# Self-attention with the scores laid the other way round: keys on the partitions, the softmax sum from a column of ones, the output normalised on its way out of PSUM

## The reference, cut to what matters

```
xn = layernorm(x, g1)
q = xn @ Wq.T                      # 16 heads of 64
kv = xn @ Wkv.T                    # one k and one v of 64
q, k = l2norm(q * 16), l2norm(k)   # each then times sqrt(16)
sim = einsum('bhid,bjd->bhij', q, k), causal
attn = softmax(sim)
out = einsum('bhij,bjd->bhid', attn, v)
out = layernorm(out @ Wout.T, g2)
x = layernorm(x + out)
```

## Time and profile before

| what | value |
|---|---|
| median of 3 executions | 832.95 us (831.18 to 836.39) |
| the profiled execution | 833.86 us |
| its span, first to last instruction | 832.1 us |
| TensorE busy / weight loads | 770.5 us (93%) / 646.4 us (78%) |
| VectorE, ScalarE, GpSimd busy | 620.7 us (75%), 596.5 us (72%), 454.3 us (55%) |
| granted TensorE clock, mean | 0.987 of full speed |

### The profile page before, as it was taken

How to read it: one execution, slowest core, us unless ns; L and a number is a source line. 1 busy time by engine, 2 the same in 40 slices (tenths; PEclk the granted TensorE clock), 3 DMA queues, 4 the chain that set the end, 5 groups by cost and what they waited for, 6 DMA issues and landing times.

```text
span 832.1 us, 26529 instructions
## 1 busy us (share of the span) xinstructions
PE 770.5 (93%) x9276; PEld 646.4 (78%) x9308; DVE 620.7 (75%) x1834; ACT 596.5 (72%) x1444; POOL 454.3 (55%) x442
## 2 busy tenths in 40 slices
PE   3799999999999998899899999999999989989995
PEld 3577778777777877788788888887888878989962
DVE  3877878878877874789888888888888965744425
ACT  2688888878878874777778777676767667767735
POOL 6467776776777672222253535444443537776643
PEclk9899999999999999999999999999999989999998
DMA  8299999100000000000000000000000227878745
GB/s 273 67 159 165 162 161 156 16 0 0 0 0 0 0 3 2 6 7 7 7 22 17 23 17 20 20 20 20 16 23 14 72 76 225 254 221 250 248 157 210
DMA packets 69392, 64.79 MB, mean 78 GB/s; under 512 B 5702, under 2 KB 54985, under 8 KB 69168
## 3 DMA queue, kind: packets, MB, share of 16 engines
q1 hardware_dynamic: 62592, 51.42, 29.8%
q0 software_dynamic: 4624, 9.61, 3.3%
q10 hardware_dynamic: 2080, 2.49, 1.0%
HBM read 35.37 MB, written 28.58 MB: 77 GB/s over the span
## 4 chain that ended last, share of the span: by engine, by line
PE 47%; issue 19%; POOL 13%; DVE 9%; ACT 6%; DMA 3%; SPq 1%; POOLq 0%; DVEq 0%; ACTq 0%
PE bank L1715 7%; PE bank L1819 6%; PE bank L1515 5%; POOL rq L534 5%; PE bank L1517 5%; PE bank L1516 5%; POOL PR L539 3%; PE bank L1829 3%; PE bank L1703 3%; PE bank L1591 2%; PE bank L1599 2%; PE bank L1690 2%; ACT VBD L393 2%; DMA w_now<-in_wl 2%; POOL rs L548 1%
## 5 line engine op out<-in xcount | busy, mean ns | idle before, releaser
L393 ACT COPY VBD<-bank 64x512 f32<-64x512 f32 x192 | 111.4, 580 | 28.1 <-PE bank L1517 25.4
L571 POOL TENSOR_TENSOR PR<-PR,rL 128x1024 f32<-128x1024 f32 x32 | 60.9, 1904 | 107.9 <-DVE rL L1125 107.7
L534 POOL TENSOR_TENSOR rq<-ssq,mhalf 128x17 f32<-128x17 f32 x32 | 99.3, 3102 | 14.4 <-DVE ssq L974 13.8
L539 POOL TENSOR_TENSOR PR<-PR,rL 128x1024 f32<-128x1024 f32 x32 | 61.0, 1905 | 82.4 <-DVE rL L1005 82.4
L638 POOL DMA_INDIRECT zbuf<-arena x71 | 69.8, 983 | 31.6 <-issue 21.2
L626 POOL DMA_INDIRECT xbuf<-xg,slot x64 | 64.9, 1013 | 34.2 <-DVE xg L1320 21.6
L1819 PE MATMUL bank<-xT,w_now 128*128 128x128 f32 x568 | 77.3, 280 | 3.1 <-DMA w_now<-in_wl 2.7
L1819 PEld LDWEIGHTS bank<-xT,w_now 128*128 128x128 f32 x568 | 70.4, 195 | 4.6 <-issue 3.5
L1446 DVE SCALAR_TENSOR_TENSOR stage<-bank,b_now,early 128x128 f32<-128x128 f32 x142 | 43.3, 347 | 40.4 <-ACT early L892 32.6
L892 ACT ACTIVATE early<-bank,b_now 128x128 f32<-128x128 f32 x142 | 44.6, 365 | 35.8 <-PE bank L1819 35.7
L1715 PE MATMUL bank<-VBD,PT 128*64 128x128 f32 x1024 | 64.7, 280 | 3.2 <-ACT PT L808 3.2
(11 more groups left out here) (253 smaller groups left out, 2296.0 us busy)
## 6 DMA issues: line engine op xcount, KB each, us to landing
w_now<-in_wl SPq DMA_DIRECT2D x71, 256.0 KB
xbuf<-blank SPq DMA_DIRECT2D x1, 17160.0 KB, 119.6
arena<-xbuf SPq DMA_DIRECT2D x71, 65.0 KB
VBD<-zbuf SPq DMA_DIRECT2D x4, 512.0 KB, 5.0
out<-X SPq DMA_DIRECT2D x8, 256.0 KB, 2.3
cT<-in_ctxT ACTq DMA_DIRECT2D x16, 96.0 KB, 1.9
zbuf<-arena POOLq DMA_INDIRECT x71
wl_sb<-in_wl POOLq DMA_DIRECT2D x1, 1024.0 KB, 8.5
```

The lines of the kernel that those rows point to most:

```text
L393: u = copy(VBD[h * SEQ:(h + 1) * SEQ, p, s, lo:lo + blocks, :], bank[CHUNK_BANK[c]][s * SEQ:(s + 1) * SEQ, :].rearrange("k (a d) -> k a d" ...
L534: nc.gpsimd.tensor_tensor(rq[:, :], ssq[:, :], mhalf[:, 0:HEADS + 1], ALU.pow).then_inc(a["pow"], 1)
L539: nc.gpsimd.tensor_tensor(v, v, rL[:, p, :].unsqueeze(2).broadcast_to([P, HEADS, SEQ]), ALU.mult)\
```

## The change

It turns the scores round. The keys stand on the partitions now: four products of 64x64 corners with 512 columns (one per sequence and half of the heads) in place of 32 with 64 columns. The exponentials then are already the stationary operand of the product with the values, so that the transposes of the weights, ScalarE's copies of them and the block diagonal `VBD` go. v has a column of ones beside it (`kvS`, a ring of VB = 4 tiles), so that the 65th column of the product is the sum over the keys. The sum on VectorE, its reciprocal over 16 heads and GpSimd's multiply go; the new `o_norm` on VectorE takes the reciprocal of those columns and multiplies the output on its way out of PSUM. It lies with the queries on the partitions, so eight transposes on TensorE and two copies on ScalarE (`o_T`) follow before the projection, which works on each sequence by itself. Beside that: x, k and kv share bank 1 (with waits on `kvS`), the square sums, powers, caps and normalise steps are done by halves of the heads, the loop has four tiles, and y of the last two tiles goes to banks 2 and 3.

```diff
 def norms(t, p):                                        # GpSimd
+    for c in range(2):
+        s = half(c)
+        pool.wait_ge(a["ssq"], 2 * t + c + 1)
...
+        nc.gpsimd.tensor_tensor(rq[:, s], ssq[:, s], mhalf[:, s], ALU.pow).then_inc(a["pow"], 1)
-def weights(t, p):
-    pool.wait_ge(a["sum"], 2 * t + 2)
...
+def kv_evac(t, p):                                      # ScalarE
     act.wait_ge(a["kv"], t + 1)
     nc.scalar.activation(wide[:, W:W + DH], bank[1][:, 0:DH], ACT.Square).then_inc(a["sq"], 1)
+    nc.scalar.activation(kvS[:, p, 0:2 * DH], bank[1][:, 0:2 * DH], ACT.Copy).then_inc(a["kvS"], 1)
...
+def o_norm(t, p):                                       # VectorE
+    dve.wait_ge(a["o"], t + 1)
+    first = psum[:, 4:6, 0:O_LAST * O_W].rearrange("q s (a d) -> q s a d", d=O_W)
+    last = psum[:, 0:2, O_AT:O_AT + O_W]
+    V.reciprocal(rO[:, :, O_LAST:NBLK], last[:, :, DH:O_W]).then_inc(a["rO"], 1)
+    V.reciprocal(rO[:, :, 0:O_LAST], first[:, :, :, DH]).then_inc(a["rO"], 1)
...
+    V.tensor_tensor(On[:, :, O_LAST, :], last[:, :, 0:DH], ...)
+    for s in range(PB):
+        V.tensor_tensor(On[:, s, 0:O_LAST, :], first[:, s, :, 0:DH], ...)
...
 def qk_T(t, p):                                         # TensorE
...
     pe.wait_ge(a["kn"], t + 1)
+    pe.wait_ge(a["kvS"], upto_tile(t + 2))
+    nc.tensor.transpose(bank[1][:, KN_AT], kn[:, :, :].rearrange("q s d -> q (s d)"), ident[:, :])\
 def scores(t, p):
...
-                m = M(bank[6 + h][s * SEQ:(s + 1) * SEQ, k * SEQ:(k + 1) * SEQ],
-                      QT[r, p, k, s * SEQ:(s + 1) * SEQ], kT[r, p, s * SEQ:(s + 1) * SEQ],
-                      start=False, stop=(k == NBLK - 1))
+            m = M(bank[6 + h][q, :], kT[r, p, q], QT[r, p, :, q], start=False, stop=True)
...
-def values(t, p, s):
-    M(bank[4 + s][:, :], VBD[:, p, s, 0, :], PT[:, s * HW:(s + 1) * HW], start=True, stop=True)\
+def values(t, p):
+    for k in range(NBLK):
...
+        for s in range(PB):
+            rows = slice(s * SEQ, (s + 1) * SEQ)
+            for h in range(2):
...
+                m = M(to[h * SEQ:(h + 1) * SEQ, :], PR[rows, p % 2, at:at + SEQ], kvS[rows, p, V_ONE],
+                      start=True, stop=True)
+def o_T(t, p, s):
+    pe.wait_ge(a["on"], 3 * t + 2 + s)
...
 # order in a turn, TensorE
-stage_of(qkv, i, p, 0)
+self_stage(q_product, i, p, 0)
+self_stage(lambda t, q: o_T(t, q, 0), i, p, 3)
+self_stage(lambda t, q: o_T(t, q, 1), i, p, 3)
+self_stage(kv_product, i, p, 0)
```

More of the change, by code:

```diff
@@ L275, in pipeline @@
             for i in range(first):
[L276 to L281, removed]
+                body(i, i % VB)
+            with eng.Fori(first // VB, T // VB - 1) as j:
+                for k in range(VB):
+                    body(VB * j + k, k)
+            for i in range(T - VB, last + 1):
+                body(i, i % VB)
         A_FIRST = 8
@@ L842, in cross @@
                 if isinstance(i, int) and i == 0:
[L843 to L848, removed]
+                    for t in (T - 2, T - 1):
+                        for s in range(PB):
+                            o_T(t, t % 2, s)
+                        y_evac(t, t % 2)
                 if (g := due(i, scores_at)) is not None:
@@ L992, in v_bd, with cap @@
[L992 to L1005 removed]
+            def cap(t, p, c):
+                dve.wait_ge(a["pow"], 2 * t + c + 1)
+                if c == 1 and later(t, 1):
+                    dve.wait_ge(a["kn"], t)
+                V.tensor_tensor(rinv[:, half(c)], rq[:, half(c)], caps[:, half(c)], ALU.min).then_inc(a["cap"], 1)
@@ L1428, in _ @@
             body(T, 0)
+            o_norm(T - 2, 0)
             def b1_column(t, q):
@@ L1561, in scores @@
                     pe.wait_ge(a["exp"], 2 * t)
-                pe.wait_ge(a["xT"], T if isinstance(t, int) and t + 3 >= T else t + 3)
+                if later(t, 2):
+                    pe.wait_ge(a["oT"], 2 * (t - 1))
                 for h in range(2):
-                    M(bank[6 + h][:, :], ident_b[:, :], causal[:, :, :].rearrange("q h k -> q (h k)"), start=True, stop=False)
-                for k in range(NBLK):
+                    M(bank[6 + h][:, :], ident_b[:, :], causal[:, :, :].rearrange("k a q -> k (a q)"), start=True, stop=False)
@@ new lines, in o_T @@
+            def o_T(t, p, s):
+                pe.wait_ge(a["on"], 3 * t + 2 + s)
+                pe.wait_ge(a["exp"], 2 * upto_tile(t + 2))
+                if later(t, 1):
+                    pe.wait_ge(a["oT"], 2 * t)
+                for g in range(HBLK):
+                    m = nc.tensor.transpose(bank[6 + s][:, g * P:(g + 1) * P],
+                                            On[:, s, 2 * g:2 * g + 2, :].rearrange("q a d -> q (a d)"), ident[:, :])
+                m.then_inc(a["oT_ps"], 1)
```

331 lines of the change are left out of this document (163 added, 168 removed).

## The result

The changed kernel takes **837.39 us** (median of 19 runs, 834.42 to 842.39) against 831.9 for the kernel before in the same runs: ratio **1.0069, 95% interval 1.0053 to 1.0085**, slower by 0.7%. The forecast was 809, range 797 to 827. The profiled execution has 835.65 and a span of 833.9.

What follows compares the result with a forecast made beforehand. TensorE was taken to bound self-attention at 9.09 us a tile, falling to 8.45. Savings of 17 (middle), 5 (start) and 2 (end) sum to 24, from 833.86 to 809.9, or 809 as median; range 797 to 827.

Steps and rivals of the forecast that it cites:

- 27 tiles between start and end x 0.64 = 17: Self-attention's middle tiles: each falls from 9.09 to 8.45 us, 0.64 less, giving 17 us over 27 tiles.
- Start (5): First self-attention tiles: half powers let q start earlier and GpSimd's multiply stall goes; 4 to 6 us, taken as 5.
- the steady 1.5 a tile: Tiles 1 to 3: the next q starts some 1.5 us earlier, with only 1.68 of power before the first half.
- End (2): End of self-attention: the 1.40 wait for GpSimd's weights and two transposing steps go, o_norm and copies stand open; 2 us saved.
- The tile (8.45): One self-attention tile: TensorE work of 8.07 plus a 0.35 wait, and VectorE's loop of 8.4 to 8.5; taken as 8.45 us.
- the wait at the k transpose: TensorE's k transpose waits for ScalarE's kv copy, which reads the same bank; 0.35 us lost a tile.
- Both loops come out alike: TensorE with ScalarE (8.4 us) and VectorE with GpSimd (8.4 to 8.5) were taken to bound a tile about equally.
- Rival 3: Scores on TensorE overlap too little, 2.1 us instead of 1.0; tile 9.5, kernel slower at 842; chance 0.10.
- strict program order: Skill page on TensorE: matmuls start and end in program order; by that rule slower scores and 842 us would follow.
- The lock between VectorE and GpSimd: Skill's port-lock rule: each half power could block a two-SBUF-input VectorE operation by up to 1.7 us; the sum kept zero.
- Rival 2: VectorE's in-order queue becomes a longer bound; tile up to 9.1 us, kernel 827, or 818 for half; chance 0.24.
- Rival 1: TensorE stays the bound, ScalarE reaching the kv copy earlier; tile 8.07 us, kernel 799, or 797; chance 0.12.

Runs made afterwards that it cites:

- late_fill: Changed kernel with the blank fill of xbuf (17160 KB) held in SyncE's queue until ten tiles have left the projection; 818.1 us, ratio 0.9802.
- before_proj_16: Kernel before, with its output projection as 16 products of 64 stationary columns (32 records) in place of 8 of 128 (16 records); 855.88 us, ratio 1.021.
- two edits: Changed kernel with the late fill, plus projection in 16 records and kv product and copies ahead of o_T on TensorE and ScalarE; 799.22 us, ratio 0.9603.
- late_kv_first: Changed kernel with the late fill and the kv product ahead of o_T on TensorE, its copies ahead of o_T's on ScalarE; 805.55 us, ratio 0.9665.

## Why the prediction was wrong, step by step

- **The step that failed is "27 tiles between start and end x 0.64 = 17".** It multiplied a tile from the middle over the whole stage. Of the 28 distances between kv products 3 and 31, the last 19 took 163.4, 2.9 more than 19 x 8.45; the first nine took 98.8 where 9 x 8.45 = 76.0 was counted. These 22.7 are nearly all of the miss: the profiled span is 833.9 where 809.9 - 1.8 = 808.1 was forecast, 25.8 more (22.7 + 2.9 + 1.2 for the end - 0.9 for a 28th tile and for 17.3 taken as 17 - 0.2 for the start; 0.1 is rounding). late_fill, which moves the fill and nothing else, brings these nine tiles to 77.1 and the kernel to 818.1.
- **What stood in its place**: TensorE waiting for packets of its own instructions beside the fill, 16.1 us. I priced TensorE's instructions by their durations, which came out close, and never by their number. The change cuts time from values and scores by many small products (values 4 records to 64, projection 16 to 32, scores 64 to 8): 8.07 us of work, but 132 records in place of 112, which the kernel before could just have brought beside the fill (9.10 a tile there, 9.08 later). The page of before showed the fill, and the first-pass tiles as fast as the others; it did not show how near they were to the limit. None of the rivals had it. Nor did I price the larger loop: tiles 10 and 11, which the kernel before runs from code it already has, took 9.97 and 10.16, some 3 us more than two of 8.55. No run has the changed kernel with a loop of two tiles, so the shares of the records and of the loop are not shown apart; before_proj_16 shows that records alone are enough.
- The Trainium skill's page "Runtime: NRT & Kernel Launch", section "Instruction fetch mechanics", has instructions come in blocks of 16 KiB of 256 instructions, fetched ahead, the cost of a block "mostly hidden". The size agrees: q8 has 10 packets and 0.16 MB, and 255 to 257 instructions stand from one wait to the next. Mostly hidden they were without the fill (no wait over 0.3 in late_fill from 38 to 137 us), and not with it: 16.1 us of idle in the same stretch.
- **Start (5)**: right in sum, 5.15, and in part by luck, for its pieces were not the steady 1.5 a tile that I added up: by the starts of the kv products, 0.5 was won up to tile 0, then 3.0, -0.1 and 1.8. **End (2)**: 0.8. The transposes that replace the wait for GpSimd's weights wait themselves for o_norm, which has no q product to hide it there; in TensorE's timeline at the end, answering to the earlier trace rows:

```profile
309.34 1.19 PE L1614 MATMUL psum<-ident,PT 128*128 128x128 f32 x8 [2.10 <-DVE PT L1008]
...
323.71 1.16 PE L1604 MATMUL psum<-kvS,PR 64*64 64x65 f32 x64 [1.05 <-issue]
```

  The second wait has no releaser, and it too ends 1.2 us after a packet of queue 8 lands (322.48), here with the fill long over.
- **The tile (8.45)**: 8.5 to 8.6, and 8.9 at every fourth, where the loop turns. Its parts were right: scores 0.91 for 1.0, values 1.04 for 1.1, o_norm 1.56 for 1.6, the wait at the k transpose and behind it 0.34 for 0.35. "Both loops come out alike" was wrong as a bound: taking that wait away gave 0.38, so VectorE's loop was not yet in the way, and with two edits TensorE runs a tile in 7.98 to 8.04.
- **Rival 3** (scores that do not overlap, 842) gives a time near the measured one, for a reason that is not there: it needed a scores step of 1.7, and the row has 0.91. The sentence on strict program order made rival 3 the outcome; that inference was wrong, whatever the order, for the step is half of the 1.7 that it needed.
- **The lock between VectorE and GpSimd** did not show: x_lo takes 0.28 at 175.18, before the second power ends (the cap behind it still waits for it until 175.86). Rival 2 did not come in the later tiles. Rival 1 did not either, but its condition, ScalarE earlier at the kv copy, is what late_kv_first makes: 8.17 for its 8.07.

What stays open: how a packet of instructions waits among the fill's own packets (the trace shows it once it moves), why before_proj_16 falls to one packet and one tile per 14 us in its tiles 3 to 6, what the 0.3 at the turn of the loop is, and two tiles of late_fill beside the fill, 9.69 and 9.42, in which TensorE waited for o_norm. That the granted clock fell after some of these stalls is in the rows; it was not tried apart from the stall.

## What to carry to other kernels

Cost an edit of a tight loop in instructions as well as in microseconds, count the tiles of an unrolled loop body with them, and look at which stretch of the program runs code for the first time: a bulk transfer that nobody needs yet can starve the engine of its instructions there, and moving it behind the first turn of the loop moved the ratio from 1.0069 to 0.9802. An idle time with no releaser in the middle of a group of equal products is the sign. Do not carry a steady tile over the whole stage before the first tiles have been held against the middle ones for every resource that differs between them.

## What the runs showed of the hardware that I had not expected

- TensorE's instructions come in packets of 16 KB on a queue of their own, about one per tile here, and a stalled TensorE went on 1.2 to 1.9 us after its packet landed. Beside a fill that moved some 160 GB/s ten of them took 99 us (changed kernel), without it 79 (late_fill).
- A loop body of four tiles (some 1,060 matmuls and loads) turned without any packet from 157 to 240 us; one of eight was fetched anew in its second turn, and its jump back waited 9.55 beside the fill.
- Behind the stall of 4.39 the granted clock stood at 0.50 from 94 to 97 us, and was back at 1.00 from 98 to 102. The clock stood at 0.50 behind one more of the nine waits of the changed kernel (1.62, then 63 to 66 us) and not behind the one of 2.83, and with four of the five in before_proj_16: such idle time can be paid for twice.
